# A decoder block on one core: the last mixture's routing done group by group inside the perceptron ahead of it

## What is computed

```
h = gelu(_ln(x_out, ln3_g, ln3_b) @ li2_w + li2_b);  x_out + h @ li3_w + li3_b      # last perceptron

def _L1_ffn_ref(x, Wr, W1, W2):                 # E, F, K = 8, 256, 2; x is layernormed
    logits = flat @ Wr.T
    weights, ids = jax.lax.top_k(logits, K)
    weights = jax.nn.softmax(weights, axis=-1)
    router_weights = zeros.at[rows, ids].add(weights)
    h = einsum('nc,efc->nef', flat, W1);  val, gate = h[..., :F], h[..., F:]
    out = einsum('nec,ne->nc', einsum('nef,ecf->nec', val * silu(gate), W2), router_weights)
```

## Time and profile before

| what | us |
|---|---|
| median of 3 runs | 3338.94 |
| lowest and highest run | 3336.98, 3344.69 |
| the profiled execution, time | 3309.97 |
| the profiled execution, span on the core | 3308.0 |

### The profile page before, as it was taken

One profiled execution on the slowest core, in us unless ns is written; L12 is line 12 of the kernel. 1 busy time (PEld: TensorE's weight loads), 2 busy tenths in 40 slices (PEclk: granted clock), 3 DMA queues, 4 the chain that ended last, 5 costly groups with the idle time before them and its releaser, 6 DMA issues. The chain is left out here.

```text
span 3308.0 us, 52202 instructions
## 1 busy us (share of the span) xinstructions
PE 2507.7 (76%) x16122; PEld 1838.5 (56%) x16123; DVE 2198.0 (66%) x4397; ACT 1525.6 (46%) x4269; POOL 898.2 (27%) x1267
## 2 busy tenths in 40 slices
PE   3888888862395999989922897999997699975085
PEld 2655665552395666656611675666665466654075
DVE  4999999972023777757767433888885489855044
ACT  4666666631021777755521232777774254432011
POOL 4334344423553000013210411111110133311754
PEclk8888888885697999999966777999998899996598
DMA  9200000000474000000000300000000000000176
GB/s 354 122 0 0 0 0 0 0 0 24 135 218 118 1 0 0 0 7 1 0 7 0 63 1 16 1 0 0 0 0 8 16 1 0 0 8 1 52 204 192
DMA packets 107793, 128.26 MB, mean 39 GB/s; under 512 B 30281, under 2 KB 80273, under 8 KB 103570
## 3 DMA queue, kind: packets, MB, share of 16 engines
q1 hardware_dynamic: 98450, 107.66, 10.6%
q0 software_dynamic: 9216, 19.02, 1.7%
HBM read 69.23 MB, written 57.41 MB: 38 GB/s over the span
## 5 line engine op out<-in xcount | busy, mean ns | idle before, releaser
L675 DVE TENSOR_TENSOR_SCAN s_state<-s_decay,s_state 128x4096 f32<-128x4096 f32 x32 | 278.0, 8687 | 35.0 <-ACT s_decay L473 35.0
L571 PE MATMUL s_ysumP<-s_state,ident 128*128 128x256 f32 x1024 | 287.8, 434 | 1.4 <-DVE s_state L685 1.4
L1169 ACT ACTIVATE s5a_prob<-s5a_scoreP,s5a_nmax 128x256 f32<-128x256 f32 x512 | 235.2, 474 | 66.0 <-DVE s5a_nmax L1343 65.6
L571 PEld LDWEIGHTS s_ysumP<-s_state,ident 128*128 128x128 f32 x1024 | 217.7, 223 | 35.4 <-DVE s_state L685 1.9
L516 PE MATMUL s_bcP<-s_bc,s_sel 96*128 96x256 bf16 x768 | 151.4, 337 | 107.6 <-DVE s_state L685 92.9
L1169 ACT ACTIVATE s2s_prob<-s2s_scoreP,s2s_nmax 128x128 f32<-128x128 f32 (+1 forms) x512 | 208.2, 423 | 45.0 <-DVE s2s_nmax L1341 43.8
L473 ACT ACTIVATE s_decay<-s_delta,s_aneg 128x255 f32<-128x255 f32 x512 | 210.0, 493 | 33.1 <-DVE s_delta L652 32.9
L2808 POOL DMA_INDIRECT parts<-m_y,m_to x160 | 153.1, 957 | 149.3 <-DVE m_y L2899 124.3
L1343 DVE TENSOR_REDUCE s5a_nmax<-s5a_scoreP 128x4 f32<-128x1024 f32 x128 | 156.6, 1223 | 44.6 <-PE s5a_scoreP L1264 42.0
L2977 PE MATMUL m_turnP<-ident,m_xin 128*128 128x128 f32 x160 | 32.7, 287 | 197.7 <-DMA m_w<-in_m_w 197.6
L516 PEld LDWEIGHTS s_bcP<-s_bc,s_sel 96*128 96x128 bf16 x768 | 82.3, 117 | 177.0 <-DVE s_state L685 125.5
(11 more groups left out here) (588 smaller groups left out, 6302.7 us busy)
## 6 DMA issues: line engine op xcount, KB each, us to landing
sorted<-blank SPq DMA_DIRECT2D x32, 1105.0 KB, 27.9
m_w<-in_m_w SPq DMA_DIRECT2D x120, 256.0 KB, 3.3
m_xin<-sorted SPq DMA_DIRECT2D x80, 130.0 KB, 2.2
m_row<-parts SPq DMA_DIRECT2D x32, 256.0 KB, 5.1
m_w<-in_m_w SPq DMA_DIRECT2D x40, 128.0 KB, 3.2
s_mats<-s_scratch SPq DMA_DIRECT2D x4, 1024.0 KB, 12.7
parts<-m_y,m_to POOLq DMA_INDIRECT x160, 3.2
sorted<-m_row,m_idx POOLq DMA_INDIRECT x128, 2.3
```

The lines of the kernel that those rows point to most:

```text
L571: ins = nc.tensor.matmul(ysumP[:, c, :], ident[:], state[s][:, c, n, :], start=(n == 0), stop=(n == NS - 1))
L675: nc.vector.tensor_tensor_scan(cells, flat(decay[c]), cells, 0.0, ALU.mult, ALU.add).then_inc(S["scanned"], 1)
L1169: ins = nc.scalar.activation(prob[i][:, h, a:b], scoreP[i][:, h, a:b], ACT.Exp, bias=nmax[:, p % 4, h, r:r + 1], accum_out=den[s][:, r, 2 ...
```

## The change

`mlp_route` (line 897 of the changed file) takes the place of the last `mlp`, and does the first part of the mixture as well; `stage56` calls it and then `sparse` with `rt`, an object that holds what outlives the perceptron: `row`, the two tables, and the semaphores `sent` and `map_ready`. With `rt`, `sparse` has no norm, no router, no `route` and no sending; it begins with SP's two waits. All eight groups are written out, no loop is left, and three more turns (t = 8, 9, 10) follow in which only the later steps run.

A group passes through four turns: perceptron up to the gelu (t), product back, `take` and norm (t+1), transpose, copy and router (t+2), choice, ranks, slots and sending (t+3). The ranks of a group need no sum over all tiles: `run` holds for each partition how many rows of earlier groups went to each expert; products with `before`, with `ones` (for the earlier tiles of the group) and of `ones` with `run` add up in one accumulation. The weights are sigmoids of the difference of the two logits. The router's transposes are written into `outP`, the perceptron's own output buffer, after `take` has read it.

```diff
+        @block.gpsimd
+        def _(pool):
...
+            for t in range(N + 3):
+                if of(t, 1):
+                    rnorm.root(nc, pool, t - 1)
+                if t + 2 < N:
+                    norm.root(nc, pool, t + 2)
+                if of(t, 3):
+                    r = t - 3
+                    pool.wait_ge(S["doubled"], r + 1)
+                    pool.wait_ge(S["shared"], 2 * r + 2)
+                    pool.wait_ge(S["slotted"], r + 1)
+                    for i in range(r * G, r * G + G):
+                        for k in range(2):
+                            nc.gpsimd.indirect_dma_start(xs, bass.IndirectOffsetOnAxis(idx[:, k, i:i + 1], 0), row[:, k, i, :],
+                                                         None).then_inc(rt.sent, 16)
...
+        @block.scalar
+        def _(ac):
...
+            for t in range(N + 3):
+                if t + 1 < N:
+                    turn_in(t + 1)
+                if t < N:
...
+                        nc.scalar.activation(act[t % 2][:, c, :], hidP[c][:], ACT.Gelu, bias=b1[:, c:c + 1]).then_inc(S["acted"], 1)
+                if of(t, 2):
...
+                    nc.scalar.activation(rowT[r % 2][:].rearrange("p (g c) -> p g c", g=G), outP[r % 2][:], ACT.Copy
+                                         ).then_inc(S["rowT_ready"], 1)
+                    nc.scalar.activation(rows(row[:, 1], r)[..., 0:C], rows(row[:, 0], r)[..., 0:C], ACT.Copy).then_inc(S["doubled"], 1)
+                if of(t, 3):
...
+                        nc.scalar.activation(row[:, k, r * G:r * G + G, C + 1], apart[r % 2][:], ACT.Sigmoid, scale=1.0 - 2.0 * k
+                                             ).then_inc(S["shared"], 1)
...
+        @block.tensor
+        def _(pe):
...
+            def ranks(r):
+                pe.wait_ge(S["chosen"], r + 1)
+                wait(pe, S["run_ready"], r)
+                nc.tensor.matmul(gateP[:, 1], before[:], both[:], start=True, stop=False, skip_group_check=True)
+                for g in range(1, G):
+                    nc.tensor.matmul(gateP[:, 1, g:G, :], ones[:], both[:, 0:G - g, :], start=False, stop=False, skip_group_check=True)
+                nc.tensor.matmul(gateP[:, 1], ones[:], run[:].unsqueeze(1).to_broadcast([P, G, E]), start=False, stop=True,
+                                 skip_group_check=True).then_inc(S["ranked"], 1)
+            turn(0)
+            pe.wait_ge(S["loaded"], 64)
+            pe.wait_ge(S["consts"], 8)
+            for t in range(N + 3):
+                if t < N:
+                    hid(t)
+                if t + 1 < N:
+                    turn(t + 1)
+                if of(t, 2):
+                    rturn(t - 2)
+                if of(t, 3):
+                    ranks(t - 3)
+                if of(t, 1):
+                    out(t - 1)
+                if of(t, 2):
+                    logits(t - 2)
...
+        @block.vector
+        def _(ve):
...
+            for t in range(N + 3):
+                if of(t, 3):
+                    choose(t - 3)
+                if t < N:
+                    carry(t)
+                if of(t, 1):
+                    take(t - 1)
+                if of(t, 3):
+                    slots(t - 3)
+                if of(t, 1):
+                    ve.wait_ge(S["out_used"], t)
+                    rnorm.stats(nc, ve, st, t - 1, lambda g: tile(xres, t - 1, g))
+                if t + 2 < N:
+                    norm.stats(nc, ve, st, t + 2, lambda g: tile(src, t + 2, g))
+                if of(t, 1):
+                    rnorm.scaled(nc, ve, st, t - 1, lambda g: tile(xres, t - 1, g), lambda g: tile(row[:, 0], t - 1, g)[:, 0:C])
...
+                if t + 2 < N:
+                    ve.wait_ge(S["turned"], t + 1)
+                    front(t + 2)
...
-def stage6(nc, xres, ident, dram):
-    sparse(nc, xres, ident, dram, "m6_", True, dram["m6_store"])
+def stage56(nc, xres, ident, dram):
+    with ExitStack() as ctx:
+        rt = Routed(Scope(nc, ctx, "m6r_"))
+        stage5(nc, xres, ident, dram, rt)
+        sparse(nc, xres, ident, dram, "m6_", True, dram["m6_store"], rt=rt)
```

More of the change, by code:

```diff
@@ L22 @@
 HOLES, BLANKS, SPILL = 17, 16, 2048
+CAP = NB * L
 def wait(eng, sem, value):
@@ L2673, in sparse @@
         wr = sc.sb("wr", [P, E])
-        norm = Norm(sc, "n_", G) if src is None else None
-        row = sc.sb("row", [P, 2, NT, D])
-        xnT = [sc.sb(f"xnT{s}", [P, G * P]) for s in range(2)]
-        col = sc.sb("col", [P, NT, E])
-        before = sc.sb("before", [P, P])
-        ones = sc.sb("ones", [P, P])
-        later = sc.sb("later", [P, E, NT])
-        start = sc.sb("start", [P, E, NT])
-        turn_w = sc.sb("turn_w", [P, E, CAP // W])
-        tile_no = sc.sb("tile_no", [P, J, E])
@@ L2684, in sparse @@
-        lg = sc.sb("lg", [P, NT, E])
-        rest = sc.sb("rest", [P, NT, E])
-        seek = sc.sb("seek", [P, NT, E])
-        hot = [sc.sb(f"hot{k}", [P, NT, E]) for k in range(2)]
-        both = sc.sb("both", [P, NT, E])
-        top = [sc.sb(f"top{k}", [P, NT, 1]) for k in range(2)]
-        which = sc.sb("which", [P, NT, 1])
-        ex = sc.sb("ex", [P, NT, 1])
-        share = sc.sb("share", [P, NT, 1])
-        tot = sc.sb("tot", [P, E, NT])
-        cum = sc.sb("cum", [P, E, NT])
-        base = sc.sb("base", [P, E, NT])
@@ L2696, in sparse @@
-        slot = sc.sb("slot", [P, NT, E])
-        at = [sc.sb(f"at{k}", [P, NT, 1]) for k in range(2)]
-        idx = sc.sb("idx", [P, 2, NT], U32)
-        full = sc.sb("full", [P, E, CAP // W])
-        count = sc.sb("count", [P, E])
-        ends = sc.sb("ends", [P, E])
-        past = sc.sb("past", [P, J, E])
-        owner = sc.sb("owner", [P, J])
-        skipped = sc.sb("skipped", [P, J])
-        place = sc.sb("place", [P, J])
-        map_row = sc.sb("map_row", [P, J], I32)
-        map_own = sc.sb("map_own", [P, J], I32)
+        norm = Norm(sc, "n_", G) if src is None and rt is None else None
@@ new lines, in sparse @@
+        row = rt.row if rt else sc.sb("row", [P, 2, NT, D])
+        if not rt:
+            xnT = [sc.sb(f"xnT{s}", [P, G * P]) for s in range(2)]
+            col = sc.sb("col", [P, NT, E])
+            before = sc.sb("before", [P, P])
+            ones = sc.sb("ones", [P, P])
+            later = sc.sb("later", [P, E, NT])
+            start = sc.sb("start", [P, E, NT])
+            turn_w = sc.sb("turn_w", [P, E, CAP // W])
+            tile_no = sc.sb("tile_no", [P, J, E])
+            lg = sc.sb("lg", [P, NT, E])
+            rest = sc.sb("rest", [P, NT, E])
+            seek = sc.sb("seek", [P, NT, E])
+            hot = [sc.sb(f"hot{k}", [P, NT, E]) for k in range(2)]
+            both = sc.sb("both", [P, NT, E])
+            top = [sc.sb(f"top{k}", [P, NT, 1]) for k in range(2)]
+            which = sc.sb("which", [P, NT, 1])
+            ex = sc.sb("ex", [P, NT, 1])
+            share = sc.sb("share", [P, NT, 1])
+            tot = sc.sb("tot", [P, E, NT])
+            cum = sc.sb("cum", [P, E, NT])
+            base = sc.sb("base", [P, E, NT])
+            slot = sc.sb("slot", [P, NT, E])
+            at = [sc.sb(f"at{k}", [P, NT, 1]) for k in range(2)]
+            idx = sc.sb("idx", [P, 2, NT], U32)
+            full = sc.sb("full", [P, E, CAP // W])
+            count = sc.sb("count", [P, E])
+            ends = sc.sb("ends", [P, E])
+            past = sc.sb("past", [P, J, E])
+            owner = sc.sb("owner", [P, J])
+            skipped = sc.sb("skipped", [P, J])
+            place = sc.sb("place", [P, J])
@@ L2903, in scale @@
                 ins.then_inc(S["scaled"], 1)
-            st.do(nc.vector.memset(ends[:], 0.0))
-            for t in turns(ve, N):
-                st.begin(t)
-                front(t)
-            st = Steps(ve, S["tail_step"])
-            route()
+            if not rt:
+                st.do(nc.vector.memset(ends[:], 0.0))
+                for t in turns(ve, N):
+                    st.begin(t)
+                    front(t)
+                st = Steps(ve, S["tail_step"])
+                route()
+            else:
+                ve.wait_ge(S["consts"], 1)
             for j, s, q, first, last in tiles(ve):
@@ L2932, in _ @@
         def _(ac):
-            for j in turns(ac, N // 2):
+            for j in turns(ac, 0 if rt else N // 2):
                 for s in range(2):
```

254 lines of the change are left out of this document (237 added, 17 removed).

## The result

The changed kernel takes 3295.52 us (median of 7 runs, 3293.9 to 3303.45) against 3335.4 us for the one before (median of 7, 3313.06 to 3344.69): a ratio of 0.989, 95% interval 0.9867 to 0.9912. The forecast was 3299, with 3281 to 3319. Against the three runs shown ahead of the prediction it is 43 us less, against the seven 40.

The account below looks back on a forecast made before the run. The stretch from the last perceptron to the next part's load was a 222 us serial chain, PE bounding the perceptron, POOL's sends 36%. Sum: -60.8 + 0.8 + 2.3 + 17.5 = -40 us off the median, 3299, range 3281 to 3319.

Parts of the forecast that it names:

- The basis: Whole kernel: the 40 us gain is taken off the timed median of 3338.94, not the profiled 3309.97, giving 3299.
- The sends: POOL: 1.263 us each; 40 of 64 leave the bare path, 24 follow the last root in 29.5 us.
- The first `take`: Start of the last perceptron: PE and DVE wait for POOL's constants, +2.4 us, so first `take` at 2946.4.
- The loop: Last perceptron, `take` to `take`: take, slots, norms, choice, ranks, product back close on themselves, 15.25 us at the upper clock.
- the clock's +17.5: Last perceptron: PE's clock falls in holes, each product back about 2.5 us later, seven of eight, +17.5; bounds 0 and 34.7.
- Handovers and PSUM, +2.3: Changed stretch: products and selects that read PSUM and some fourteen more handovers cost +2.3 us, bounds 0 and 6.
- The barrier: Stage's end: barrier falls into the sends' landing; 3.84 us from last send's start to the next part's first load.
- PE idle ahead of the ranks: Last perceptron, expected sign: PE stands idle ahead of its ranks, ended by `both` of DVE; no size given.
- Rival 1: Last perceptron: the clock does not fall because transposes in the hole suffice; -57.7 us, 3281; chance 0.2.
- Rival 2: Last perceptron: DVE and POOL exclude each other, loop 27 us instead of 17.8; +17 us, 3356; chance 0.04.
- Rival 3: Last perceptron: PE stays at 1.2 GHz from ranks to router in all loops; -23 us, 3316; chance 0.2.
- Rival 4: Last perceptron: roots wait behind eight sends on in-order POOL; 3310 with slower sends, near no change with half exclusion; chance 0.06.

Follow-up runs that it names:

- e5_before: The kernel before the change, unedited, profiled once more; the profiled execution took 3328.92 us.
- e3_sends_last: Changed kernel with all 64 sends moved behind the last root; 3343.99 us, 1.0025 of the kernel before.
- e1_after: Changed kernel without any edit, run again beside the others; 3298.0 us, 0.9887 of the kernel before.
- e9_fill_last: Changed kernel with unread PE products in all three holes of a turn and all 64 sends behind the last root; profiled execution alone, 3332.32 us.
- e6_fill: Changed kernel with PE products that nobody reads in all three holes of a turn; 3297.32 us, 0.986 of the kernel before.
- e7_drain: Changed kernel with POOL waiting for its sends to land before the stage's end; 3295.06 us, 0.9863 of the kernel before.
- e2_bank: Changed kernel with the router's products put into the product back's spent bank, without the wait for slots; 3296.5 us, 0.9884 of the kernel before.
- e8_early: Changed kernel with product back ahead of transposes and ranks, router results copied by ScalarE, gelu and slots reordered; 3270.78 us, 0.9787 of the kernel before.
- e10_probe: Changed kernel with all sends last and eight rounds of unread PE products beside them, their ends marked by ACT; profiled execution alone, no time given.
- e11_probe2: As e10_probe, but four sets of four 512 column products first, then 8 and 128 column kinds, all twice; 3378.98 us profiled, 3369.73 the other execution.

## Why the prediction was right, point by point

The way from load to load, in the prediction's terms and in the profile of the changed kernel:

| part | predicted | measured |
|---|---|---|
| stage's first load to first `take` | 26.1 | 29.8 |
| first to last `take`, with clock and handovers | 118.1 | 116.0 |
| last `take` to the end of the last root | 4.5 | 4.3 |
| to the start of the last send | 29.5 | 29.5 |
| to the next part's first load | 3.8 | 8.7 |
| sum | 182.0 | 188.4 |

- **The basis.** The prediction took its difference off the median, since the 29 us between it and the profiled execution were in no place that it could name. e5_before shows where most of them lay: 17 are a tail that was short by chance. The other 12 stay unplaced.
- **The sends.** Right: 1.263 each, 24 in a row behind the last root, 40 off the bare path (e3_sends_last).
- **The first `take`.** 3.7 too early. PE waits for POOL's constants as said (its first product starts 9.15 us into the stage; it was 6.57), but the second group's first product takes 6.65 at the lower clock where it took 3.67. In e1_after it took 3.67 again, and the part is 26.6.
- **The loop.** Its parts are right: `take` to `both` 9.8 (said 10.3), ranks and product back 4.99 (said 4.95). In e9_fill_last, with clock up and no sends, the whole turn is 14.8 (said 15.25). The loop closes where it was said to.
- **The step that failed is the clock's +17.5 as the sole cause.** The 2.5 us a turn are there, and the clock does fall in each turn, as the earlier trace rows had it. But with the clock held up the turn keeps them (e6_fill), and with the sends away and a fall it is 16.4 to 16.8. From first to last `take` it is 97.2 us with neither cause (e9_fill_last; said 98.2), 105.3 with the fall alone (e3_sends_last), 111.0 with the sends and the fillers (e6_fill), and 111.5 and 116.0 with both (e1_after and the first profile). So the fall alone is worth 8 us and the sends alone some 14, and together they give 14 to 19, less than their sum. The term of 17.5 lies in that range, but half of what it stands for was put on the wrong cause. The size was luck in that part.
- **Handovers and PSUM, +2.3.** The middle turns have no room for them. The scope that closes at the end cost 0.7 of the 0.8 allowed: from the last sum's end to the output's DMA 1.75 us (3290.36 to 3292.11), before 1.04 (3297.46 to 3298.50).
- **The barrier.** "The stage's barrier falls into the landing" was wrong: the load comes 4.8 us later than counted, and by e7_drain the landing is no part of it.
- **The wait for the slots** was missed, and costs nothing (e2_bank).
- **PE idle ahead of the ranks**: 1.47 us in e1_after, none in the turn shown above, where the first product ran at the lower clock and filled the hole. Part of PE's idle time lies ahead of the router's product instead, behind the slots.
- **Rival 1** (no fall, 3281): the clock fell, and e6_fill says that it would not have given 3281 anyway. **Rival 2** (DVE and POOL in turns): DVE's small instructions are as short as ever, `take` to `both` is 9.8 in e1_after with sends and in e9_fill_last without. **Rival 3**: ranks to `take` never took the 9.9 of the lower clock all through. **Rival 4**: the root found POOL idle in every turn. What came instead was a rival that was not listed, sends against the signals of PE.
- **A sign of being wrong that came.** "If sends beside DVE took over 1.3 each": three in the changed kernel did, 1.45 to 1.46 each, beside `carry`. POOL is idle for over 4 us ahead of its roots then, so it cost nothing.

## What to carry to other kernels

In these runs, work put beside a row of GpSimd's DMAs had to be priced by its number of TensorE instructions too, where another engine waits for its end. The price was 2.5 us beside eight sends and 1.40 us an instruction beside a long row, so a product of many small pieces loses most. Where a chain of engines closes on itself, look first for the link that can be taken out (the product back needed no choice), which gave 24 to 27 us (together with the smaller moves of e8_early), while the fillers for the clock gave nothing as long as the sends stood there. And a stage that ends with such DMAs pays for leaving it, so let it end with other work.

## What the hardware showed that was not expected

- Beside a long row of indirect sends TensorE's signals come out at one instruction in 1.40 us, until 7 us after the last send. TensorE runs on until it is 63 instructions ahead of them and is then held to the same pace (e10_probe, e11_probe2). The Trainium skill, SBUF — State Buffer, section "Who interferes with whom", says that PE and ACT never wait on anyone. For SBUF's ports that may hold, and the runs don't say which resource it is; as a rule for planning, the measurement speaks against it.
- The recorded end of a product is not when others see it. `take` stood up to 3.0 us behind it (e6_fill), and a mark up to 65 us (e10_probe). The Trainium skill, Perfetto Trace Analysis, section "Tensor Engine Instruction (MATMUL, LD_WEIGHTS)", says that the end is computed from the instruction's size, not observed. No run here shows the end itself; marks on another engine show when it is known there.
- A send that stands beside DVE's sums of two SBUF operands takes 1.45 to 1.46 us instead of 0.96 (3019.21 in the changed kernel, 3014.73 in e1_after); the sums stay at 0.69. The Trainium skill, SBUF — State Buffer, section "Who interferes with whom", says that two SBUF inputs of DVE contend with a GpSimd instruction that reads SBUF; the trace agrees. Beside scalings and small instructions sends take 0.95 to 1.20, so the full stop of rival 2 is not seen.
- POOL's DRAIN behind sends lasts 5.3 us from the last send's end in the changed kernel, and 5.29 when all sends have landed before it (e7_drain).
